# Scores four pairs ahead of the exponents instead of seven, in a transformer layer on one core

## What is computed

```
q, k, v = shape(h @ Wq.T), shape(h @ Wk.T), shape(h @ Wv.T)
scores = einsum('bhqd,bhkd->bhqk', q, k) * SCALING + position_bias
attn = softmax(scores, axis=-1)
ctx = einsum('bhqk,bhkd->bhqd', attn, v)
x = x + ctx @ Wo.T
...
x = x + ffn(layernorm(x))
```

## Time and profile before

| what | value |
|---|---|
| median of 3 runs | 864.57 us (864.25 to 865.86) |
| the profiled execution | 863.94 us, of which the span from first to last instruction is 862.1 us |
| PE busy | 769.9 us, 89% of the span |
| DVE busy | 615.8 us, 71% |
| ACT busy | 477.2 us, 55% |
| POOL busy | 259.5 us, 30% |
| stage `attend` | from 111.8 us to about 530 us of the span |

### The profile page before, as it was taken

The page is one execution under the profiler, slowest core; times in us unless marked ns, Lnnn a source line. Parts: engine busy times, 40 slices in busy tenths (PEclk is TensorE's granted clock), DMA queues, the critical chain, the costliest instruction groups (busy, mean ns, idle before and its releaser), DMA issues. The chain is left out here.

```text
span 862.1 us, 18204 instructions
## 1 busy us (share of the span) xinstructions
PE 769.9 (89%) x6177; PEld 537.0 (62%) x6177; DVE 615.8 (71%) x1907; ACT 477.2 (55%) x720; POOL 259.5 (30%) x405
## 2 busy tenths in 40 slices
PE   4879878999999999999999997799999889999910
PEld 2768636666666666666665564556664489999910
DVE  5567377888888888888888851576674457777745
ACT  2334304666666666666666673464554267777700
POOL 1111011121112111111112110267567326666620
PEclk9989956999999999999999999799998999999975
DMA  4899783553356334553355633555422445555369
GB/s 120 239 349 333 256 234 96 141 141 106 102 152 167 109 99 129 165 141 93 104 158 162 202 114 142 153 167 183 142 86 80 141 132 159 160 161 161 124 246 381
DMA packets 74486, 140.73 MB, mean 163 GB/s; under 512 B 14504, under 2 KB 34624, under 8 KB 74222
## 3 DMA queue, kind: packets, MB, share of 16 engines
q1 hardware_dynamic: 64434, 119.52, 45.6%
q0 software_dynamic: 9792, 19.54, 6.9%
q10 hardware_dynamic: 172, 0.56, 0.3%
HBM read 85.70 MB, written 56.78 MB: 165 GB/s over the span
## 5 line engine op out<-in xcount | busy, mean ns | idle before, releaser
L721 DVE CUSTOM_DVE_ANT_0 sums<-pS,near 128x512 bf16<-128x512 f32 x512 | 329.5, 688 | 54.2 <-PE pS L783 45.8
L754 ACT ACTIVATE prob<-pE 128x1024 f32<-128x1024 f32 x256 | 248.5, 1022 | 154.8 <-PE pE L808 154.7
L808 PEld LDWEIGHTS pE<-bandT,place 64*128 64x128 f32 x2048 | 167.1, 190 | 12.5
L808 PE MATMUL pE<-bandT,place 64*128 64x244 f32 (+2 forms) x2048 | 164.4, 272 | 0.0
L783 PE MATMUL pS<-k_st,q_st 48*128 48x512 f32 x512 | 140.1, 479 | 10.6 <-DVEq L707 7.7
L783 PEld LDWEIGHTS pS<-k_st,q_st 48*128 48x128 f32 x512 | 63.8, 194 | 120.4 <-DVE nmax L721 88.9
L822 PE MATMUL pC<-prob,v_aug 128*32 128x512 f32 x1024 | 135.8, 604 | 1.0 <-ACT ctx_sb L762 1.0
L800 PE MATMUL pE<-q_st,k_st 62*128 62x512 f32 x512 | 115.3, 405 | 1.8 <-DMA q_st<-negated_maxima 1.1
L1055 POOL DMA_INDIRECT expert_rows<-rb,xr x76 | 84.1, 1106 | 57.0 <-DVE rb L1233 45.1
L1039 POOL DMA_INDIRECT routed_rows<-xr,slot_i x64 | 65.4, 1022 | 46.1 <-DVE slot_i L1167 27.4
L1510 PE MATMUL pD<-w2p,hT 128*128 x456 | 63.5, 289 | 0.4 <-DVE hT L1226 0.4
(11 more groups left out here) (169 smaller groups left out, 1040.4 us busy)
## 6 DMA issues: line engine op xcount, KB each, us to landing
xr<-routed_rows SPq DMA_DIRECT2D x38, 258.0 KB, 2.9
q_parts<-qk SPq DMA_DIRECT2D x16, 512.0 KB, 5.4
k_parts<-qk SPq DMA_DIRECT2D x16, 512.0 KB, 5.1
q_st<-q_parts SPq DMA_DIRECT2D x64, 128.0 KB, 2.8
k_st<-k_parts SPq DMA_DIRECT2D x64, 128.0 KB, 2.9
ctx<-ctx_sb SPq DMA_DIRECT2D x32, 256.0 KB, 2.7
near<-bias_by_distance SPq DMA_DIRECT2D x16, 448.0 KB, 5.0
xr<-expert_rows SPq DMA_DIRECT2D x12, 512.0 KB, 7.4
```

What stands on the lines that cost most here:

```text
L721: dve.tensor_tensor_reduce(sums[:, r % 4], pS[:, unit % PS], near[:, hg % 2, j, lead:lead + S], -1.0, BIG, ALU.add, ALU.min, nmax[:, j, t: ...
L754: act.activation(prob[:, par, 2 * step:2 * step + 2], pE[:, 2 * (step % 2):2 * (step % 2) + 2], ACT.Exp).then_inc(exp_done, 1)
L808: ins = pe.matmul(pE[:, bank + side, a:z], place[rows, half], bandT[rows, (quad // 2) % 2, pair, part, lead:lead + z - a], start=False, st ...
```

## The change

```
         STEPS = HPG // 2 * TT
-        LEAD = 7
+        LEAD = 4
```

## The result

The changed kernel takes 916.45 us (median of 4 runs, 913.02 to 921.75) against 865.22 us for the kernel before (4 runs, 864.25 to 868.84): a ratio of 1.0588, 95% interval 1.0553 to 1.0623. The forecast was 906 us, in a range of 887 to 938. The profiled executions stand at 916.86 and 863.94 us, 52.9 apart. Direction and range held. The way to the sum did not: the forecast wanted every slot about 1.1 us longer, and the trace has 19 slots nearly as short as before and ten long ones. Two of the forecast's own signs failed with it: 17 of 29 stores come 12.2 to 12.9 us after the one before instead of 13.4, and the clock does not stay at 1.00.

The account below looks back on a forecast made before the run. PE sets the pace; the maxima's DRAM trip, hidden before, would exceed its room. Slots 1 to 29 +30.7, slot 0 +0.6, slot 30 +3.1, last slots +7: +41.4 on 863.94 gives 905.3, median 906 us; range 887 to 938.

Parts of the forecast that it names:

- the forecast's own signs: In the new trace: about 30 read-back waits at L800, 30 to 50 us; stores 13.4 us apart; clock 1.00 from 163 us.
- start and slot 0: Stage start unchanged, 0; in slot 0, at the lower clock, the next X at 149.0 in place of 148.40 us, +0.6.
- slots 1 to 29: Every such slot takes 13.39 us in place of 12.33 because PE waits for the maxima, together +30.7 us.
- the last slots: Near the stage's end, next-stage loads slow the maxima's way through DRAM in five or so slots; half of some 15 us, +7.
- slot 30: It took 10.29 us with scores only in its first step; now it takes as long as the others, +3.1 us.
- The room: Time from turned maxima, X + 7.02 us, to the next X: 5.1 us, against 9.9 before.
- The trip: The maxima's way through DRAM, from transposition's end to PE's start: 6.4 us, so PE waits some 1.3 us once a pass.
- Even the best of every part: With the lowest store and load landings in the earlier trace, a slot still takes 12.92 us, above 12.33.
- the ring: Each slot as a closed chain through all engines, first exponents to turned maxima and back through DRAM: 7.02 + 6.37 = 13.39 us.
- rival 2: Maxima's transfers stay as crowded or get worse, SP's next-slot loads starting ahead of the second read-back; some 945 us, chance 12%.
- A wait of 1.3 us is like the first: PE's wait resembles the 0.98 us pause at 526.47 us, around which the clock kept 0.99, so the clock stays up.
- rival 4: TensorE's clock falls at every wait, a slot takes some 17 us and the kernel about 1000 us; chance 2%.

Follow-up runs that it names:

- early_readback: Changed kernel (LEAD = 4), but POOL reads back pass 0's maxima for every pass, ahead of the store, so no slot waits for its store; 864.6 us, ratio 0.999.
- shift32: Changed kernel (LEAD = 4) plus 32 short useless matmuls on PE ahead of slot 0, so each instruction fetch comes 3.1 us earlier; 898.26 us, ratio 1.0383.
- shift12: Changed kernel (LEAD = 4) plus 12 short useless matmuls on PE ahead of slot 0, so each instruction fetch comes 1.2 us earlier; 918.3 us, ratio 1.0624.
- lead3: Changed kernel with LEAD = 3 in place of 4; 993.62 us, ratio 1.149 to the kernel before.
- late_loads: LEAD = 4 kernel with `near` loads cut to 16 KB, 32 useless matmuls, and next-stage loads moved to SP's last slot; 891.69 us, ratio 1.0312.

## Why the prediction was right and where it was wrong

| term | forecast | measured |
|---|---|---|
| start and slot 0 | +0.6 | -1.5 |
| slots 1 to 29, ordinary (19) | 29 x 1.06 = +30.7 | +6.1 |
| slots 1 to 29, nine long ones | in the term above | +35.4 |
| the last slots | +7 | +10.4 (one slot) |
| slot 30 | +3.1 | +2.2 |
| slot 31 and `finish` | 0 | +0.3 |
| sum | +41.4 | +52.9 |

The measured terms come from X, the first exponents of a pass, on PE and its weight loads, which answer to the earlier trace rows:

```profile
131.93 0.80 PE L800 MATMUL pE<-q_st,k_st 62*128 62x512 f32 x2 [4.39 <-DMA q_st<-negated_maxima]
...
146.89 0.21 PEld L800 LDWEIGHTS pE<-q_st,k_st 62*128 62x128 f32 x2 [0.76 <-issue]
...
555.41 0.19 PEld L800 LDWEIGHTS pE<-q_st,k_st 62*128 62x128 f32 x2
...
567.93 0.21 PEld L800 LDWEIGHTS pE<-q_st,k_st 62*128 62x128 f32 x2 [2.32 <-issue]
```

Slots 1 to 29 take 555.41 - 146.89 = 408.5 us against 504.97 - 148.40 = 356.6. The nine long ones hold 146.1 of it, less 9 x 12.30 makes +35.4; the one of 22.67 makes +10.4; the rest is the 19 others, and half of it, 3.1 us, lies in the two beside the late store no. 26.

- *Start and slot 0.* No loss at the start, as said; the 0.6 us of slot 0 did not come, it took 14.96 us (131.93 to 146.89) for 15.21. Of the 1.5 us gained 1.2 are the execution's and not the change's: PE's first scores of the stage already stand at 110.68 us instead of 111.87, before anything that was moved. Fewer scores ahead of the first exponents only lengthened PE's wait there, to 4.39 us.
- *The room.* Right. Maxima turned at X + 7.02 were forecast; 6.93 and 6.95 us measured wherever the clock holds. early_readback shows that nothing but the trip uses it up.
- *The trip in ordinary slots.* Wrong, and the step that failed first: "Even the best of every part ... is 12.92 us, still above 12.33". The store was never alone in the trace of before; its 2.6 us were 0.4 to 0.6 above what it takes in the new place. With 0.30 + 2.30 + 0.55 + 2.0 + 0.15 = 5.3 us and 6.95 the ring is 12.25 us, no longer than PE's own work. A lowest value among 27 slots of one order is no lower bound for another place in the slot.
- *One ring length for all slots.* Wrong, and this is what the number owes its luck to: an ordinary slot that was too dear and long slots that were not foreseen came to nearly the same sum. A term of 1.06 in each of 29 slots was in truth 0.3 in 19 and 3.9 in nine. As the trip just fits, each delay counts in full and draws others along. In the slot from 307.21 us the store is 2.2 us late by the instruction fetch, the read-backs 0.8 by SP's loads, which is how rival 2 was meant; 0.30 + 4.48 + 0.55 + 2.8 + 0.15 = 8.3 us of trip. shift32 and shift12 show the first by moving it; the second is read from the trace alone. Over the nine long slots, against an ordinary slot (2.30 us from store to first read-back, 2.72 on to the weight loads, 6.95 on to turned maxima), the late stores make 18 us, the later read-backs 6.5 and the lower clock 11, together the 35 of the table. This is a sum read from one trace, not an experiment.
- *The clock.* "A wait of 1.3 us is like the first" was not put to the test, since hardly a wait had that size: the ordinary slots wait 0.6 us or less, and the clock stays at 1.00 from 154.13 to 241.80 us. In the long slots the waits are 2.1 to 4.3 us, and behind seven of the nine the clock dropped for a few microseconds, which adds 1.5 to 2.0 us from X to turned maxima. So rival 4 is right in part: a drop in part of a slot and not in all of it, and not in every slot. The rule of the Trainium skill named beside it (TensorE: Matmul & The Clock Gate, "HAM oscillation — how this bites in real kernels") has every tile start at the lower clock after its wait; the trace agrees for those seven waits and not for the two of 2.58 and 2.80 us at 283.81 and 315.02 us. lead3's slots show the drop as a cost of its own for LEAD at 3; with LEAD at 4 no experiment sets it apart from the late landings.
- *The last slots.* The mechanism was right, late_loads shows it; it is one slot with +10.4 us in place of five that share 7. I took half of the excess of 3.4 us that the earlier trace rows show; there POOL waited 5.62 us, here 6.50. Against an ordinary slot the store is 4.9 us late here, the read-backs, with 5.1 to 5.7 us, add 3.4, and the lower clock 2.0.
- *Slot 30 and `finish`.* As forecast within 1 us. It is one execution against one; their medians lie 51.2 us apart, the profiled ones 52.9.

My expectations for LEAD 5 and 6 failed on the same point as the forecast: they were made from the ordinary slot, while the loss comes from the few trips that are longest.

Left open: why the fetch, once it stands 0.1 to 0.4 us behind a store's first packets, stays there for six slots in a row (a longer slot moves both), and what shifts it by 1 to 1.7 us at the start and end of such a row. It was seen to shift near where a new group of heads starts, and nothing was tried on it.

None of the eleven kernels is faster than the kernel before, and nothing in them points to one that would be: at LEAD 7 the room of 9.9 us covers the trips of its own trace (the longest, has 6.32 us from store to read-back), and more lead brings nothing.

## What to carry to other kernels

Where a trip through DRAM is hidden, compare its slack with the longest trips in the trace, not with the median: 19 of 29 slots lost 0.3 us each here, the other ten 46 in all. Look at which transfers stand beside it at the new point of time, instruction fetches included: here they came about once a slot, so that one met the store in six slots in a row. A loop that only just fits makes a late landing, a later issue behind other loads and a lower clock add up in the same slot.

## What the hardware did that I had not expected

- PE's instructions arrive by DMA in pieces of 16 KB, one about every slot, and the store of the maxima, when one starts 0.1 to 0.4 us behind its first packets, lands in 3.6 to 4.2 us instead of 2.0 to 2.3.
- The 16 KB store to DRAM and the loads of 8 KB from it land in 1.9 to 2.0 us at best; nothing in the trace of before showed the store under 2.6.
- The clock dropped behind seven of eleven pauses of 2.1 to 4.3 us, among them one of 2.12, and not behind one of 3.06. Matmuls of no use in such pauses made the kernel with LEAD at 3 17 us faster, in part because they moved the fetch.
- 32 matmuls of no use ahead of the loop made this kernel 18 us faster, 12 of them did not.
- POOL issues one store, no. 26, 2.2 us after its maxima are turned instead of 0.3, so 1.9 us late, in every kernel looked at (at 489.71 us in the changed one), and no engine or transfer is named for it. With LEAD at 7 it is hidden.
